# An RWKV layer with a gated FFN on 8 cores: first transfers, prologue order and the first units of token chunk 1

## The chip, the cores and the metric

The kernel runs on one Trainium2 chip, on all 8 NeuronCores, with one program. Core b takes batch element b and shares nothing with the others but the memory that the weights are read from. A core has a matrix engine (PE), a vector engine (DVE), a scalar engine (ACT), a general engine (POOL), a queue engine that only starts transfers (SP), and 16 DMA engines that all queues feed. The metric is the device time in microseconds of the slowest core.

## What is computed

Each core has x of 4096 tokens by 1024 channels.

```python
xn = _layernorm(x, axis=-1)
x = x + attn(xn) + ffn(xn)

# attn: k = xn Wk^T, r = xn Wr^T, v = r, w = -exp(time_decay), u = time_first
y = wkv_scan(w, u, k, v)          # a recurrence over the tokens, by channel
out = sigmoid(r) * y
attn = out @ Wo^T

# ffn, weights of integers times 1/127, hidden size 3072
ffn = (silu(xn @ Wgate^T) * (xn @ Wup^T)) @ Wdown^T
```

## The kernel before

**Chunks and units.** The tokens are cut into 8 chunks of 512 (`TC`), each of 4 tiles of 128 tokens (`NT`). A *unit* of projection work is two accumulation groups of 8 matmuls of 512 columns, into the two banks of one of three PSUM pairs (`pair`). A "gu" unit is 128 hidden channels of gate (line 309) and up (line 313); a "kr" unit is 128 channels of k (line 309) and r (line 313). Its weight tile is 1 MB of int32 or float32 in memory, is cast to a bfloat16 tile of 512 KB by a POOL transfer (line 262), and goes to one of four ring buffers (`R = 4`). Chunks 0 and 1 are worked in pairs, so that each weight tile is read once for both: `GU` and `KR` list the units in order, and `gu 0, 1, 2` are chunk 0 and `gu 3, 4, 5` are the same three weight tiles for chunk 1. SP writes each cast tile back to memory in bfloat16 (line 200) for chunks 2 to 7.

**Layer norm of a tile.** SP loads 128 rows of x (`x_load`, line 170, 512 KB). DVE takes the statistics (`ln_bn`: two `BATCH_NORM_STATS2` and an aggregate), ACT makes the reciprocal deviation (`ln_rstd`: Ln, drain, Exp), DVE the bias (`ln_nb`), ACT the normalised tile (`ln_xt`, line 381, into one of two `xt` buffers). PE transposes it with 8 matmuls of 128 columns (`tr`, line 291), and ACT and DVE copy one bank each into `xn` (`ln_ev`, lines 397 and 503). Chunks 0 and 1 (tiles 0 to 7) are done so in the prologue.

**After a unit.** For a gu unit ACT takes the silu of the gate bank (`gate`, line 420) and DVE multiplies (`ffn_h`, line 549, which raises `v_h` and so frees the PSUM pair). For a kr unit DVE takes the maximum (`att_max`), ACT three exponentials (`att_exp`), DVE the product (line 521, which raises `v_zA` and frees the pair) and two scans (`att_scan`), then `att_den`, ACT the reciprocal (`att_rec`: Ln and Exp), and DVE `att_out`. There is one buffer each of `ek`, `zA` and `den`.

**What sets the order.** Every engine's stream is written out by hand, and waits are on counting semaphores. `SLOTS` lists what takes the PSUM pairs in turn: slot q uses pair q % 3, and `acquire` waits until slot q - 3 has been read. Before the change the transposes have slots too. PE's prologue is `tr(0..3)`, gu 0, `tr(4)`, gu 1, `tr(5)`, gu 2, `tr(6)`, `tr(7)`, kr 0, and from there on three gu units and a kr unit in turn. SP issues x tiles 0 to 7, the two small tables `tdt` and `tft`, and three tiles of x for the residual sum (`res_load`), all without a wait. POOL waits for x tile 3 (`xl3`, line 255) and then issues the first four weight tiles; a later one waits for its ring buffer (`unit_done`) and for the write-back of what was in it (`wb_done`). After the projections of chunks 0 and 1 come, by chunk, the output units (lines 327 and 334) and the projections of the later chunks.

## Time and profile before

| | before |
|---|---|
| time, median of 3 runs | 1359.35 us (1358.83 to 1359.63) |
| the profiled execution's own time | 1359.52 us |
| its span, slowest core (core 3) | 1358.0 us |
| spans of cores 0 to 7 | 1356.6, 1357.7, 1356.3, 1358.0, 1355.6, 1357.1, 1357.8, 1357.7 us |
| PE busy | 1334.7 us (98%) |
| DVE, ACT, POOL busy | 674.6, 396.5, 35.2 us |
| granted TensorE clock, all cores | 1.00 |

The span goes from the first to the last instruction of a core. The time of the execution is 1.5 us longer than the span of its slowest core. A PE that is 98% busy leaves some 23 us in which it is not, and the 40 slices of the page put nearly all of that into the first slice. So the views to read are those of the prologue: the chain of waits, the instructions in order of time, and the transfers.

### The profile page before, as it was taken

To read this page: it belongs to the slowest core of one execution; us is meant where nothing else is said; L and a number is where in the kernel's file an instruction comes from. 1 tells how busy PE (TensorE), PEld (TensorE's weight loads), DVE (VectorE), ACT (ScalarE), POOL (GpSimd) and SP (SyncE) were. 2 spreads that over 40 slices of the span, in tenths; PEclk is the share of its full clock that TensorE was granted. 3 is DMA by queue.
4 is the path that set the end of the run, shared out by engine and by line. 5 is a ranking of instruction groups with operands and counts; after the bars stand their busy time and mean duration, and the time that the engine had idled before them with its cause. 6 is when DMAs were issued, how large, how long until landed. Compare 5 with 4: busy or idle time off the path is not lost.

```text
span 1358.0 us, 17854 instructions; the slowest of 8 cores (1355.6 to 1358.0 us)
## 1 busy us (share of the span) xinstructions
PE 1334.7 (98%) x6208; PEld 606.6 (45%) x6208; DVE 674.6 (50%) x1101; ACT 396.5 (29%) x663; POOL 35.2 (3%) x70
## 2 busy tenths in 40 slices
PE   4999999999999999999999999999999999999999
PEld 2444444444444444444444444444444444444444
DVE  4666666515952288323873238721487215672211
ACT  5554545312331233212332123221233212221100
POOL 0111111000000000000000000000000000000000
PEclk9999999999999999999999999999999999999999
DMA  9699989953554544545545444544455443334411
GB/s 231 144 183 196 209 163 181 204 142 120 167 144 148 168 137 135 147 150 176 125 117 163 155 156 124 143 152 156 150 143 126 155 155 124 94 102 164 153 47 55
DMA packets 90376, 200.41 MB, mean 148 GB/s; under 512 B 32816, under 2 KB 35888, under 8 KB 90160
## 3 DMA queue, kind: packets, MB, share of 16 engines
q1 hardware_dynamic: 55584, 167.81, 39.0%
q0 software_dynamic: 9360, 25.17, 12.5%
q10 hardware_dynamic: 25344, 6.29, 2.5%
q8 instruction: 51, 0.84, 0.2%
q14 instruction: 37, 0.30, 0.1%
HBM read 184.56 MB, written 33.55 MB: 161 GB/s over the span
## 4 chain that ended last, share of the span: by engine, by line
PE 98%; DMA 2%; SPq 0%; issue 0%; DVE 0%; DVEq 0%; POOLq 0%
PE ps L309 33%; PE ps L313 33%; PE ps_o L327 24%; PE ps_o L334 8%; DMA ring<-w_gu 1%; DMA x_buf<-x_tm 1%; PE ps L291 0%; SPq L170 0%; DVE xres L556 0%; DVEq L555 0%; POOLq L255 0%
## 5 line engine op out<-in xcount | busy, mean ns | idle before, releaser
L309 PE MATMUL ps<-xn,ring 128*128 128x512 bf16 x2048 | 485.5, 380 | 4.1 <-DMA ring<-w_gu 3.9
L313 PE MATMUL ps<-xn,ring 128*128 128x512 bf16 x2048 | 484.7, 379 | 0.0
L549 DVE SCALAR_TENSOR_TENSOR h_act<-ps,silu 128x512 bf16<-128x512 f32 x192 | 132.5, 690 | 438.4 <-PE ps L313 427.5
L327 PE MATMUL ps_o<-wd_bf,h_act 128*128 128x512 bf16 x1536 | 342.0, 379 | 0.0
L309 PEld LDWEIGHTS ps<-xn,ring 128*128 128x128 bf16 x2048 | 200.5, 98 | 246.1 <-issue 6.2
L313 PEld LDWEIGHTS ps<-xn,ring 128*128 128x128 bf16 x2048 | 200.7, 98 | 242.6 <-issue 1.7
L420 ACT ACTIVATE silu<-ps 128x512 f32<-128x512 f32 x192 | 114.6, 597 | 452.7 <-PE ps L309 452.4
L327 PEld LDWEIGHTS ps_o<-wd_bf,h_act 128*128 128x128 bf16 x1536 | 150.3, 98 | 181.3
L334 PE MATMUL ps_o<-wo_bf,outp 128*128 128x512 bf16 x512 | 120.9, 379 | 0.0
L402 ACT ACTIVATE den<-den 128x512 f32<-128x512 f32 x64 | 40.3, 630 | 260.1 <-DVE den L537 259.9
L556 DVE TENSOR_TENSOR xres<-xres,ps_o 128x512 f32<-128x512 f32 x64 | 44.0, 688 | 87.0 <-PE ps_o L334 86.4
L523 DVE TENSOR_TENSOR_SCAN SAB<-ewv,SAB,zA 128x512 f32<-128x512 f32 x64 | 82.3, 1285 | 5.9
L525 DVE TENSOR_TENSOR_SCAN SAB<-ewv,SAB,ek 128x512 f32<-128x512 f32 x64 | 80.6, 1260 | 0.0
L509 DVE TENSOR_REDUCE kmax<-ps 128x1 f32<-128x512 f32 x64 | 44.0, 688 | 72.9 <-PE ps L309 72.9
L334 PEld LDWEIGHTS ps_o<-wo_bf,outp 128*128 128x128 bf16 x512 | 50.1, 98 | 60.4
L521 DVE TENSOR_TENSOR zA<-ek,ps 128x512 f32<-128x512 f32 x64 | 43.9, 686 | 15.0 <-ACT enr L413 15.0
L531 DVE SCALAR_TENSOR_TENSOR den<-ek,euv,SAB 128x512 f32<-128x512 f32 x64 | 48.1, 752 | 6.1 <-issue 0.4
L533 DVE SCALAR_TENSOR_TENSOR zA<-zA,euv,SAB 128x512 f32<-128x512 f32 x64 | 47.7, 746 | 0.0
L537 DVE SCALAR_TENSOR_TENSOR den<-enr,den 128x512 f32<-128x512 f32 x64 | 44.3, 692 | 5.2
L543 DVE TENSOR_TENSOR outp<-zA,den 128x512 bf16<-128x512 f32 x64 | 44.0, 688 | 4.9 <-ACT den L404 4.9
L488 DVE BATCH_NORM_STATS2 bnst<-x_buf 128x6 f32<-128x512 f32 x56 | 35.8, 682 | 16.7 <-DMA x_buf<-x_tm 16.7
L411 ACT ACTIVATE ek<-ps,nm 128x512 f32<-128x512 f32 x64 | 42.8, 669 | 0.0
(40 smaller groups left out, 319.1 us busy)
## 6 DMA issues: line engine op xcount, KB each, us to landing
ring<-gu_bfd SPq DMA_DIRECT2D x144, 512.0 KB, 3.3
ring<-kr_bfd SPq DMA_DIRECT2D x48, 512.0 KB, 3.9
xres<-x_tm SPq DMA_DIRECT2D x64, 256.0 KB, 5.5
out_tm<-xres SPq DMA_DIRECT2D x64, 256.0 KB, 4.7
x_buf<-x_tm SPq DMA_DIRECT2D x28, 512.0 KB, 6.4
ring<-w_gu POOLq DMA_DIRECT2D x24, 512.0 KB, 11.3
gu_bfd<-ring SPq DMA_DIRECT2D x24, 512.0 KB, 7.4
ring<-w_kr POOLq DMA_DIRECT2D x8, 512.0 KB, 7.4
```

Of the source, the lines that this page charges most:

```text
L309: ins = te.matmul(bank(kind, idx, 0), w[:, gc * D:(gc + 1) * D], xn[c % 2][:, gc, :], start=(gc == 0), stop=(gc == G - 1))
L313: ins = te.matmul(bank(kind, idx, 1), w[:, C + gc * D:C + (gc + 1) * D], xn[c % 2][:, gc, :], start=(gc == 0), stop=(gc == G - 1))
L327: te.matmul(ps_o[i % 2], h_act[c % 2][:, hg * TC + tt * D:hg * TC + (tt + 1) * D], wd_bf[:, half, hg * 512:(hg + 1) * 512], start=(hg == 0 ...
L334: ins = te.matmul(ps_o[i % 2], outp[c % 2][:, g * TC + tt * D:g * TC + (tt + 1) * D], wo_bf[:, half, g * 512:(g + 1) * 512], start=False, ...
L420: sc.activation(out=silu[i % 3], in_=bank("gu", i, 0), func=Act.Silu, scale=1.0 / 127.0).then_inc(sem["s_sil"], 1)
L509: ve.reduce_max(kmax[:, g:g + 1], bank("kr", a, 0), axis=AX)
L523: ve.tensor_tensor_scan(out=SAB[:, 0, 1:TC + 1], data0=ewv[:, g:g + 1].to_broadcast([D, TC]), data1=zA, initial=SAB[:, 0, 0:1], op0=Alu.mu ...
L525: ve.tensor_tensor_scan(out=SAB[:, 1, 1:TC + 1], data0=ewv[:, g:g + 1].to_broadcast([D, TC]), data1=ek, initial=SAB[:, 1, 0:1], op0=Alu.mu ...
L531: ve.scalar_tensor_tensor(out=den, in0=ek, scalar=euv[:, g:g + 1], in1=SAB[:, 1, 0:TC], op0=Alu.mult, op1=Alu.add)
L533: ve.scalar_tensor_tensor(out=zA, in0=zA, scalar=euv[:, g:g + 1], in1=SAB[:, 0, 0:TC], op0=Alu.mult, op1=Alu.add)
L537: ve.scalar_tensor_tensor(out=den, in0=enr, scalar=1.0, in1=den, op0=Alu.add, op1=Alu.mult).then_inc(sem["v_den"], 1)
L549: ve.scalar_tensor_tensor(out=h_act[c % 2][:, hg * TC:(hg + 1) * TC], in0=bank("gu", i, 1), scalar=1.0 / (127.0 * 127.0), in1=silu[i % 3], ...
```

## The change

Four things change, all but one before the first kr unit.

*Transfers.* SP issues x tiles 0 to 3 at once, tiles 4 and 5 when tile 3 has landed, tiles 6 and 7 when the second weight tile has; the three residual tiles come after the write-back of weight tile 8. `tdt` and `tft` are issued by ACT, as its first instructions. POOL starts the first four weight tiles when x tile 1 has landed instead of x tile 3.

*PSUM.* The transposes leave `SLOTS`. They use the output banks `ps_o` and, for tiles 1 and 3, pair 2; each bank of a transpose is waited for by itself.

*PE.* The first three gu units of chunk 1 are split by tokens, in `gu_part`: tokens 0 to 255 right after gu 2, between the transposes 6 and 7, and tokens 256 to 511 behind that. kr 0 and kr 1 follow, one behind the other. From gu 6 on the order is as before.

*DVE and ACT.* The statistics, bias and normalisation of a tile follow one another by tile, `etd` and `wv` are made at the start, and tiles 6 and 7 come behind the first gates. `att_max(1)` stands behind `att_den(0)`.

```diff
-SLOTS = [("tr", l0) for l0 in range(NT)]
-SLOTS += [("gu", 0), ("tr", 4), ("gu", 1), ("tr", 5), ("gu", 2), ("tr", 6), ("tr", 7), ("kr", 0)]
-for s0 in range(1, 2 * G):
+SLOTS = [("gu", i0) for i0 in range(6)] + [("kr", 0), ("kr", 1)]
+for s0 in range(2, 2 * G):
...
+        def tr_bank(l, k):
+            return pair[2][k] if l in (1, 3) else ps_o[k]
...
-                for l in range(2 * NX):
+                for l in range(NX):
                     x_load(l)
-                sy.dma_start(out=tdt, in_=td_hbm).then_inc(sem["io_td"], 16)
-                sy.dma_start(out=tft, in_=tf_hbm).then_inc(sem["io_tf"], 16)
-                for i in range(3):
-                    res_load(i)
+                sy.wait_ge(*x_landed(3))
+                x_load(NX)
+                x_load(NX + 1)
+                sy.wait_ge(*loaded(1))
+                x_load(NX + 2)
+                x_load(NX + 3)
...
+                            if n == 8:
+                                for i in range(3):
+                                    res_load(i)
...
-                gp.wait_ge(sem["xl3"], 16)
                 for n in range(NS):
+                    if n == 0:
+                        gp.wait_ge(*x_landed(1))
...
+                def evacuated(l, k):
+                    te.wait_ge(sem["v_ev" if k else "s_ev"], l + 1)
...
                 def tr(l):
-                    acquire("tr", l)
                     te.wait_ge(sem["s_xt"], l + 1)
                     for cb in range(G):
+                        if l >= 2 and cb % 4 == 0:
+                            evacuated(l - 2 if l < 5 else l - 1, cb // 4)
...
+                def gu_part(i, t0, t1):
+                    c = GU[i][0]
+                    if t0 == 0:
+                        acquire("gu", i)
+                        te.wait_ge(*loaded(RING_AT[("gu", i)]))
+                    w = ring[RING_AT[("gu", i)] % R]
+                    for m in range(2):
+                        for gc in range(G):
+                            if m == 0 and gc % 4 == 0:
+                                evacuated(NT * c + t1 - 1, gc // 4)
+                            ins = te.matmul(bank("gu", i, m)[:, t0 * D:t1 * D],
+                                            w[:, m * C + gc * D:m * C + (gc + 1) * D],
+                                            xn[c][:, gc, t0 * D:t1 * D],
+                                            start=(gc == 0), stop=(gc == G - 1))
+                        if t1 == NT:
+                            ins.then_inc(sem["t_u" if m else "t_g"], 1)
...
                 proj("gu", 2, 0, "t_g", "t_u")
+                gu_part(3, 0, 2)
                 tr(6)
+                gu_part(4, 0, 2)
                 tr(7)
-                proj("kr", 0, 0, "t_k", "t_r")
-                xn_ready(1)
-                for s in range(1, 2 * G):
+                gu_part(5, 0, 2)
+                for i in range(3, 6):
+                    gu_part(i, 2, NT)
+                for s in range(2):
+                    proj("kr", s, s, "t_k", "t_r")
+                for s in range(2, 2 * G):
```

Three places show how the engines' streams move. In the names, `ps0_0` is the first bank of pair 0, `ps_o0` an output bank, `ring0` a ring buffer; the semaphores `xl3` and `xl1` are the landing of x tiles 3 and 1, `ldc0` that of the first weight tile, and `v_h`, `v_zA` the freed pairs.

PE behind gu 2, before: the two transposes, kr 0, then the first unit of chunk 1.

```order
L291 MATMUL ps0_0<-ident,xt0 128x128 [waits v_h,s_xt]
L291 MATMUL ps0_0<-ident,xt0 128x128 x3
L291 MATMUL ps0_1<-ident,xt0 128x128 x4
L291 MATMUL ps1_0<-ident,xt1 128x128 [waits s_ev,v_ev,s_xt]
L291 MATMUL ps1_0<-ident,xt1 128x128 x3
L291 MATMUL ps1_1<-ident,xt1 128x128 x4
L309 MATMUL ps2_0<-xn0,ring3 128x512 [waits v_h,ldc3]
L309 MATMUL ps2_0<-xn0,ring3 128x512 x7
L313 MATMUL ps2_1<-xn0,ring3 128x512 x8
```

PE behind gu 2, after: half a unit, transpose 6, and the next half.

```order
L331 MATMUL ps0_0<-xn1,ring0 128x256 [waits v_h,ldc0,s_ev]
L331 MATMUL ps0_0<-xn1,ring0 128x256 x3
L331 MATMUL ps0_0<-xn1,ring0 128x256 [waits v_ev]
L331 MATMUL ps0_0<-xn1,ring0 128x256 x3
L331 MATMUL ps0_1<-xn1,ring0 128x256 x8
L295 MATMUL ps_o0<-ident,xt0 128x128 [waits s_xt,s_ev]
L295 MATMUL ps_o0<-ident,xt0 128x128 x3
L295 MATMUL ps_o1<-ident,xt0 128x128 [waits v_ev]
L295 MATMUL ps_o1<-ident,xt0 128x128 x3
L331 MATMUL ps1_0<-xn1,ring1 128x256 [waits v_h,ldc1,s_ev]
```

Transpose 6 now stands behind half a unit, and kr 0 is no longer behind transpose 7.

ACT behind the first transposed tile of chunk 1, before: `xt` of tile 6 (`xt0`) comes after one gate.

```order
L420 ACTIVATE silu0<-ps1_0 128x512 [waits t_g]
L397 CAST xn1<-ps2_0 128x4x128 [waits t_tr]
L381 ACTIVATE xt0<-wd_bf,nbias0,rstd0 128x1024 [waits t_tr,v_nb]
L420 ACTIVATE silu1<-ps0_0 128x512 [waits t_g]
L397 CAST xn1<-ps1_0 128x4x128 [waits t_tr]
L381 ACTIVATE xt1<-wd_bf,nbias1,rstd1 128x1024 [waits t_tr,v_nb]
L420 ACTIVATE silu2<-ps2_0 128x512 [waits t_g]
```

ACT at the same place, after: tile 6 comes behind all three gates, with its reciprocal deviation.

```order
L446 ACTIVATE silu0<-ps0_0 128x512 [waits t_g]
L423 CAST xn1<-ps_o0 128x4x128 [waits t_tr]
L446 ACTIVATE silu1<-ps1_0 128x512 [waits t_g]
L446 ACTIVATE silu2<-ps2_0 128x512 [waits t_g]
L396 ACTIVATE lnv0<-mv0,eps_t 128x1 [waits v_bn]
L398 ACTIVATE rstd0<-lnv0 128x1
L407 ACTIVATE xt0<-wd_bf,nbias0,rstd0 128x1024 [waits t_tr,v_nb]
```

The Ln and Exp of tile 6 moved from ahead of the first gate to behind the third.

PE behind the first three units of chunk 1, after: kr 0 and kr 1, then gu 6 to gu 8. Before, only kr 1 stood here.

```order
L313 MATMUL ps0_0<-xn0,ring3 128x512 [waits v_h,ldc3]
L313 MATMUL ps0_0<-xn0,ring3 128x512 x7
L317 MATMUL ps0_1<-xn0,ring3 128x512 x8
L313 MATMUL ps1_0<-xn1,ring3 128x512 [waits v_h,ldc3]
L313 MATMUL ps1_0<-xn1,ring3 128x512 x7
L317 MATMUL ps1_1<-xn1,ring3 128x512 x8
L313 MATMUL ps2_0<-xn0,ring0 128x512 [waits v_h,ldc0]
L313 MATMUL ps2_0<-xn0,ring0 128x512 x7
L317 MATMUL ps2_1<-xn0,ring0 128x512 x8
L313 MATMUL ps0_0<-xn1,ring0 128x512 [waits v_zA,ldc0]
L313 MATMUL ps0_0<-xn1,ring0 128x512 x7
L317 MATMUL ps0_1<-xn1,ring0 128x512 x8
```

The unit behind these, gu 8, takes the pair of kr 1 and waits for `v_zA` of kr 1; before, two units stood between a kr unit and the one that takes its pair as well, but no other kr unit came right ahead of it.

## Rows read from the trace of the kernel before

**Rows 1.** Waits of PE over the whole span, core 3: total us, times, longest.

```profile
PE ps L291 <- ACT xt L381: 16.0, 4, 11.5
PE ps L309 <- DMA ring<-w_gu: 3.9, 1, 3.9
PE ps L309 <- issue: 0.2, 1, 0.2
```

**Rows 2.** Chain that ended last, core 3, 0 to 42 us: start, us, what.

```profile
2.44 9.43 DMA x_buf<-x_tm
...
12.48 11.33 DMA ring<-w_gu
...
23.94 3.57 PE ps L309 x8
27.51 2.55 PE ps L313 x8
30.06 0.45 PE ps L291 x8
30.51 1.73 PE ps L309 x8
```

**Rows 3.** Instructions in order of time, core 3, layer norm: start, us, engine, line.

```profile
5.83 1.29 DVE L488 BATCH_NORM_STATS2 bnst<-x_buf 128x6 f32<-128x512 f32 x2 [4.46 <-DMA x_buf<-x_tm]
...
7.48 1.28 ACT L370 ACT_TABLE_LOAD   x1 [7.48 <-DVE mv L491]
...
8.78 0.29 ACT L370 ACTIVATE lnv<-mv,eps_t 128x1 f32<-128x1 f32 x1
9.14 0.20 ACT L372 ACTIVATE rstd<-lnv 128x1 f32<-128x1 f32 x1
...
9.47 0.15 DVE L497 SCALAR_TENSOR_TENSOR nbias<-mv,rstd 128x1 f32<-128x1 f32 x1
...
10.12 1.22 ACT L381 ACTIVATE xt<-x_buf,nbias,rstd 128x1024 bf16<-128x1024 f32 x1
...
11.49 1.01 PE L291 MATMUL ps<-ident,xt 128*128 128x128 bf16 x8 [11.49 <-ACT xt L381]
...
12.61 0.69 DVE L503 CAST xn<-ps 128x512 bf16<-128x512 f32 x1 [1.42 <-PE ps L291]
```

**Rows 4.** Chain that ended last, core 0, 18 to 25 us.

```profile
22.10 0.56 issue
```

**Rows 5.** Landing of the x tiles, line 170, core 3, 0 to 70 us.

```profile
DMA to landing us min/median/max: 4.7/10.0/13.0
```

**Rows 6.** Instructions in order of time, core 3: the gate of gu 2.

```profile
36.23 0.60 ACT L420 ACTIVATE silu<-ps 128x512 f32<-128x512 f32 x1
```

**Rows 7.** Instructions in order of time, core 3, 40 to 55 us: work behind kr 0.

```profile
40.91 0.69 DVE L509 TENSOR_REDUCE kmax<-ps 128x1 f32<-128x512 f32 x1 [1.05 <-PE ps L309]
41.67 0.16 DVE L511 SCALAR_TENSOR_TENSOR nm<-kmax,nm 128x1 f32<-128x1 f32 x1
...
43.21 0.29 ACT L409 ACTIVATE esb<-nm 128x1 f32<-128x1 f32 x1
...
44.67 0.69 DVE L521 TENSOR_TENSOR zA<-ek,ps 128x512 f32<-128x512 f32 x1 [0.78 <-ACT enr L413]
...
46.65 1.26 DVE L525 TENSOR_TENSOR_SCAN SAB<-ewv,SAB,ek 128x512 f32<-128x512 f32 x1
...
48.60 0.75 DVE L531 SCALAR_TENSOR_TENSOR den<-ek,euv,SAB 128x512 f32<-128x512 f32 x1
...
50.17 0.69 DVE L537 SCALAR_TENSOR_TENSOR den<-enr,den 128x512 f32<-128x512 f32 x1
...
53.87 0.63 ACT L404 ACTIVATE den<-den 128x512 f32<-128x512 f32 x1
```

**Rows 8.** Chain that ended last, core 1, 0 to 42 us.

```profile
24.84 3.16 PE ps L309 x8
```

**Rows 9.** Instructions in order of time, core 1, POOL.

```profile
13.11 1.76 POOL L262 DMA_DIRECT2D ring<-w_gu  x3 [11.30 <-DMA x_buf<-x_tm]
```

## What the change should do to the time: the prediction

> **What bounds the kernel now.** I read the waits of PE first. Over the whole span PE waits in three places only: 16.0 us for normalised tiles before the first four transposes, 3.9 us for the first weight tile, and 0.2 us of its own issue [rows 1]. All of it lies before 39 us; no weight tile after the first is ever waited for. So an edit can gain only by letting PE begin its first projection earlier, and whatever PE waits anew counts in full. The chain that ended last shows what sets that beginning, 23.94 us: four x tiles land by 11.87, POOL, which waits for the last of them, issues the first weight tile at 12.48, and it lands 11.33 later, at 23.81 [rows 2]. From there PE runs without a gap that matters to the end. Its first unit takes 3.57 + 2.55 us where a later one takes 2 x 1.73: 2.7 us more, since its matmuls start at half the rate [rows 2]. I leave that as it is.
>
> **The earlier weight tile.** POOL now waits for x tile 1. DVE can start on that at about 8 us, so the first weight tile is issued some 4.4 us sooner. With the same 11.33 us to landing it is there at 19.4 or, with x tiles 4 to 7 and the residual tiles no longer ahead of it, sooner. The weight tile stops being the last to come; what comes last instead is the layer norm of tile 3.
>
> **The layer norm of tiles 0 to 3.** DVE now finishes a tile before it starts the next. One tile's round is: statistics, 5.83 to ACT's start at 7.48, 1.65 us; Ln and Exp, 8.78 to 9.34, 0.56; the bias 0.15 and hops of about 0.15 [rows 3]. That is 2.5 us a tile. Making `etd` early moves ACT's table load of 1.28 us [rows 3] beside the first statistics, if `tdt` has landed by about 5.9; I take that as so. Tile 3's statistics then start at 5.83 + 3 x 2.5 + 0.7 (the cast of tile 0 ahead of it) = 14.0, when it has long landed (11.87). Onward: 1.65 + 0.56 + 0.25 to the bias, 16.5; the normalisation 0.1 + 1.22, 17.8; hop and transpose 0.15 + 1.01, 19.0; the cast 0.1 + 0.69, 19.8 [rows 3]. The new code also puts more single waits in PE's stream. On core 0 PE starts 0.56 us after the last cast ended [rows 4], with four waits behind one another there, so 0.14 each; two or three of them give 0.3. First projection at **20.1 us**, against 23.94: 3.8 us gained. The bound on the other side is the weight tile still last at 11.33 + 8.4 = 19.7, which is no later.
>
> **Transposes 6 and 7.** From 20.1, gu 0, tr 4, gu 1, tr 5, gu 2 take 6.12 + 0.45 + 3.45 + 0.45 + 3.45 = 13.9 [rows 2]: gu 2 ends at 34.0. Half a unit later, at 35.75, PE wants transpose 6. But ACT makes tile 6 ready only behind the gate of gu 2. A gate starts 0.1 after the first half of its unit and takes 0.60 [rows 6]: 33.0. Then the table of Ln and Exp must be loaded again, 1.28, the pair 0.56, DVE's bias 0.25, the normalisation 1.32 and the hop 0.15 [rows 3]: 36.55. A new wait of **0.8 us**. Tile 7's statistics follow on DVE at 35.1, and 1.65 + 0.56 + 0.25 + 1.32 + 0.15 later, at 39.0, transpose 7 can start; PE is there at 36.55 + 0.45 + 1.73 = 38.75: **0.3 us**. Behind these wait the half units of gu 4 and 5. Before, both tiles had their statistics and their reciprocal deviation done ahead of the first gate, and PE waited for neither.
>
> **The half units.** 96 matmuls of 256 columns take the place of 48 of 512. Columns are the same; a transpose matmul of 128 columns goes through in 0.45 / 8 = 0.056 us [rows 2] with its own weight load, so a load for 256 columns is hidden. I take 0 for them, and 0.3 us for waits between them, bounded by 0 and by 0.14 for each of the ten or so, 1.4.
>
> **kr 1 right behind kr 0.** gu 8 takes the pair of kr 1 and waits for its product `zA`. In the clock of the trace before, kr 0's first half ends just before 40.91 and kr 0 at 42.5; kr 1, gu 6 and gu 7 end 10.4 later, at 52.9. DVE and ACT have: maximum to 41.83, product of kr 0 to 45.36, scans to 47.91, then the `den` group, 48.60 to 50.86 in the trace, 2.26 long, now at once: 50.2. Only then comes the maximum of kr 1 (0.92): 51.2. ACT first owes the reciprocal of kr 0, two activations of 0.63 from 50.3: 51.65. From the start of the exponentials to the product are 43.21 to 44.67, 1.46, and the product takes 0.69 [rows 7]: 53.8, and PE goes at 53.9. New wait: **1.0 us**. The units behind it find their pairs free by 0.2 us or more, and the lag is gone by kr 3. Before, a kr unit had three gu units between it and the next, and PE did not wait there [rows 1].
>
> **Transfers in the rest.** The residual tiles now load beside later weight tiles. Since none of those was waited for [rows 1], I take 0, from 0 to 1.5 us. The weight tiles for gu 8 and kr 2 have two to three us more than before between issue and use, as kr 1 and the half units stand there.
>
> **The sum**, on core 3: 3.8 gained; 0.8 + 0.3 + 0.3 + 1.0 lost, and the 0.2 of issue gone: net 1.6 us, a span of 1356.4. The metric is the slowest core. Cores that did not wait for a weight tile gain less, as core 0 shows, where the cast was last [rows 4], and the slow start of PE has another length on each: on core 1 its first eight matmuls took 3.16, not 3.57 us [rows 8]. With spans of 1356 to 1357 on most cores, I put the slowest at 1356.9, 1.1 below the 1358.0 before. The profiled execution took 1359.52 for a median of 1359.35, so I carry the difference over: **1358.2 us**. A change of 0.2% is 2.7 us, about what a measurement of this kernel can tell from none; the forecast is within it.
>
> **Rivals.**
> *The new waits do not come* (17%). If tile 6 is ready in time and kr 1's product too, only the gain at the start is left, 3.8 on core 3 and some 3.5 at the slowest: 1355.6. For it: both waits are short, under 1.1 us, beside chains of ten steps. Against it: each chain is a sum of rows, and the table load alone is larger than the wait at transpose 6.
> *The weights slow x tiles 2 and 3* (15%). The weight tiles are now issued at 8 us while x tiles 2 and 3 are still in flight. On core 3 tile 3 has 2 us to spare (11.87 against 14.0). On core 1 it landed at 13.1, as POOL's issue shows [rows 9]; two streams over the same 16 engines from 10 us on would put it at 16.1, and from there 6.1 us go to the first projection: 22.2, where it was 24.84 [rows 8]. Core 1 gains 2.6 and loses 2.4: nothing is left, and by it the time is 1359.3, up to 1361 if the tile is later still.
> The Trainium skill, "DMA: Bandwidth & Descriptors", in its section "Queues, rings and completion order", has each DMA engine go round the queues it has work for, a packet at a time; by that, early weights do take bandwidth from the x tiles, and core 1's case is the rule rather than the exception. No row of before has both in flight in this stretch, so it stays a rival.
> *Tiles 6 and 7 late* (7%, slower). They are issued only when weight tile 1 has landed, by estimate some 3 us behind the first, 22 to 23, and share the engines with weight tiles 2 and 3 and two write-backs. An x tile took 4.7 to 13.0 us to land [rows 5]. At 13.0 tile 6 is there at 35.5, and 1.65 + 0.56 + 0.25 + 1.32 + 0.15 later, at 39.4, its transpose, 2.9 behind the forecast. It decides from a landing at 37.5 on: then transpose 6 is 4.9 late and the time 1363.
> *The first weight tile does not come sooner* (3%): the start stays at 23.9, the new waits stay too: 1361.6.
> *The forecast* has 58%.
>
> **How the numbers follow.** Faster by over 0.2% is below 1356.6: the first rival and a tail of the forecast, 0.20. Slower by over 0.2% is above 1362.1: the third rival, a bit of the fourth, 0.08. Same: 0.72. The range leaves the far ends of the first and the third out: 1355.6 to 1361.2.
>
> **What would show it.** First projection on core 3 near 20 us, released by a cast and not by a weight tile. A wait of PE before transpose 6 released by ACT `xt`, with a table load right ahead on ACT, 0.8 us. A wait of about 1 us on the second gu unit behind gu 6, released by DVE line 554 (`zA`). If PE waits at the half units for DMA, or x tile 3 lands after 14 us, the second or third rival holds. If ACT's first table load still stands behind the first statistics, `tdt` came late and the start is up to 1.3 us later. If the sum of PE's new waits is under 1 us, I was too dear and the change is faster.

## The result, and the profile after

The change makes the kernel slower.

| | before | after |
|---|---|---|
| median | 1359.49 us | 1366.31 us |
| range of the runs | 1358.83 to 1359.96 | 1365.91 to 1366.48 |
| ratio, 95% interval | | 1.005 (1.0033 to 1.0068) |
| span, slowest core | 1358.0 us (core 3) | 1364.7 us (core 5) |
| spans of the eight cores | 1355.6 to 1358.0 | 1362.1 to 1364.7 |

The forecast was 1358.2 us with a range up to 1361.2; the time lies 8.1 us above the one and 5.1 above the other. All medians and ranges, here and below, leave out the executions in which the cores of one die or both ran some per cent slower at a lower granted clock, whatever the kernel.

Waits of PE over the whole span, kernel after, core 5: total us, times, longest. There were six in [rows 1]; here are nine:

```profile
PE ps_o L295 <- ACT xt L407: 15.2, 4, 8.7
PE ps L295 <- ACT xt L407: 5.3, 2, 3.2
PE ps_o L295 <- ACT xn L423: 1.5, 1, 1.5
PE ps L313 <- DVE zA L554: 1.1, 1, 1.1
PE ps L313 <- DVE xn L536: 1.0, 1, 1.0
```

The same core in order of time, the steps that the prediction spoke of:

```profile
9.43 1.76 POOL L268 DMA_DIRECT2D ring<-w_gu  x3 [7.62 <-DMA x_buf<-x_tm]
...
11.62 10.92 SPq L170 DMA_DIRECT2D wd_bf<-x_tm  x4
...
20.70 3.57 PE L313 MATMUL ps<-xn,ring 128*128 128x512 bf16 x8 [1.05 <-DVE xn L536]
...
23.44 1.29 DVE L521 BATCH_NORM_STATS2 bnst<-wd_bf 128x6 f32<-128x512 f32 x2 [3.00 <-DMA wd_bf<-x_tm]
...
27.59 0.61 PE L295 MATMUL ps_o<-ident,xt 128*128 128x128 bf16 x8 [1.51 <-ACT xt L407]
...
28.41 1.29 DVE L521 BATCH_NORM_STATS2 bnst<-wd_bf 128x6 f32<-128x512 f32 x2 [2.41 <-DMA wd_bf<-x_tm]
...
33.12 0.61 PE L295 MATMUL ps_o<-ident,xt 128*128 128x128 bf16 x8 [1.46 <-ACT xn L423]
```

The first projection starts at 20.70, released by a cast and no longer by a weight tile; on the eight cores it is 20.27 to 20.75, where it was 22.30 to 24.84. That part came as forecast. Then DVE waits for x tiles 4 and 5, which [rows 1 to 3] gave no hint of: in the kernel before, the statistics of these two start at 15.44 and 18.48 on core 3 with no wait. Here they start at 23.44 and 28.41, and PE waits 1.51 us before transpose 4 and 1.46 before transpose 5.

The third new wait is the largest. What leads to transpose 6:

```profile
31.07 1.24 ACT L407 ACTIVATE xt<-wd_bf,nbias,rstd 128x1024 bf16<-128x1024 f32 x1 [0.42 <-DVE nbias L530]
...
32.41 0.56 ACT L423 CAST xn<-ps_o 128x512 bf16<-128x512 f32 x1
32.99 1.28 ACT L446 ACT_TABLE_LOAD   x1
...
34.28 0.60 ACT L446 ACTIVATE silu<-ps 128x512 f32<-128x512 f32 x1
...
36.26 0.68 DVE L582 SCALAR_TENSOR_TENSOR h_act<-ps,silu 128x512 bf16<-128x512 f32 x1
36.86 1.28 DVE L521 BATCH_NORM_STATS2 bnst<-wd_bf 128x6 f32<-128x512 f32 x2
...
38.49 1.28 ACT L396 ACT_TABLE_LOAD   x1 [2.14 <-DVE mv L524]
...
40.78 1.24 ACT L407 ACTIVATE xt<-wd_bf,nbias,rstd 128x1024 bf16<-128x1024 f32 x1 [0.43 <-DVE nbias L530]
...
42.28 1.01 PE L295 MATMUL ps_o<-ident,xt 128*128 128x128 bf16 x8 [3.35 <-ACT xt L407]
...
43.08 3.62 PE L331 MATMUL ps<-xn,ring 128*128 128x256 bf16 x16
```

Late tile 5 holds ACT, ACT's cast and table load hold the first gate, the gates hold DVE's `ffn_h`, and DVE takes the statistics of tile 6 only behind two of them. From the statistics of tile 5 to transpose 6 it is 13.86 or 13.87 us on each of the eight cores, though tile 5's statistics start anywhere from 26.99 to 28.94, and PE waits 3.35 us on each. So transpose 6 comes 13.87 us behind the statistics of tile 5, whatever PE did before. The half unit behind it takes 3.62 us; the one ahead of it took 1.91. The granted clock says why (stretch, its length, busy time and instructions by engine, then PEclk, the DMA share and GB/s):

```profile
38.00:42.00 4.00, 0.92 (x9) 0.59 (x6) 2.40 (x7) 3.00 (x4) 0.00 (x0) 0.92 0.00 0
42.00:43.00 1.00, 0.72 (x8) 0.75 (x9) 0.20 (x1) 0.52 (x3) 0.00 (x0) 0.50 0.00 0
43.00:46.50 3.50, 3.50 (x20) 2.44 (x19) 0.85 (x2) 1.71 (x2) 0.00 (x0) 0.50 0.00 0
46.50:50.00 3.50, 3.50 (x30) 3.06 (x29) 0.69 (x1) 0.59 (x1) 0.00 (x0) 0.76 0.00 0
50.00:54.00 4.00, 4.00 (x40) 3.58 (x38) 1.29 (x2) 2.37 (x3) 1.28 (x3) 1.00 0.00 0
```

PE had stood still for 3.35 us before transpose 6, and the granted clock is 0.50 (1.2 GHz) from there to 46.5, and 1.00 (2.4 GHz) again from 50. The page of the profile has the same in its first line: PE is busy 1337.5 us where it was 1334.7, with the same columns.

Last, the unit behind gu 6 and gu 7, as forecast:

```profile
69.83 1.89 PE L313 MATMUL ps<-xn,ring 128*128 128x512 bf16 x8 [1.09 <-DVE zA L554]
```

**Where the time went.** From start to start of PE's groups in the two traces, core 5 after against core 3 before (each the slowest of its kernel):

| stretch of PE | before | after | difference |
|---|---|---|---|
| start of the first projection | 23.94 | 20.70 | -3.24 |
| gu 0, up to transpose 4 | 5.96 | 6.89 | +0.93 |
| transpose 4 to transpose 5 | 3.90 | 5.53 | +1.63 |
| standing still before transpose 6 | 0 | 3.54 | +3.54 |
| transpose 6 to kr 0 | (9.64 at full clock) | 12.48 | +2.84 |
| rest, up to the end of kr 0 and gu 3 to 5 | | | -0.21 |
| wait before gu 8 | 0 | 1.09 | +1.09 |
| sum | | | +6.58 |

The 9.64 are 2 transposes of 0.46, a half unit of 1.74 and 64 matmuls in 6.98 us, as an experiment below shows them at full clock. The spans differ by 6.7. On this pair of cores the start gained 3.2 us, on core 3 alone 3.67 of the 3.8 forecast, and 9.8 us were lost behind it. The ledger says where PE lost time, not which edit made it lose it; for that there are the experiments.

### The profile page after: what moved, and what is told of

It reads as the page before. It is cut to its first block, busy times and chain, and to the rows that moved or that the text cites. A ratio compares the mean times of both kernels' runs of the same rounds, so it can differ in the third digit from the quotient of the medians.

```text
span 1364.7 us, 17958 instructions; the slowest of 8 cores (1362.1 to 1364.7 us)
## 1 busy us (share of the span) xinstructions
PE 1337.5 (98%) x6256; PEld 612.5 (45%) x6256; DVE 674.9 (49%) x1101; ACT 396.4 (29%) x663; POOL 35.1 (3%) x70
## 4 chain that ended last, share of the span: by engine, by line
PE 96%; DMA 2%; ACT 1%; DVE 1%; issue 0%; DVEq 0%; SPq 0%; ACTq 0%
PE ps L313 31%; PE ps L317 31%; PE ps_o L348 24%; PE ps_o L355 8%; DMA wd_bf<-x_tm 1%; PE ps L331 1%; DMA x_buf<-x_tm 1%; DVE bnst L521 0%; PE ps_o L295 0%; SPq L170 0%; DVE zA L554 0%; DVEq L523 0%; ACT xt L407 0%; DVE SAB L556 0%; ACT L396 0%
## 5 line engine op out<-in xcount | busy, mean ns | idle before, releaser
L313 PE MATMUL ps<-xn,ring 128*128 128x512 bf16 x2024 | 479.8, 380 | 2.1 <-DVE zA L554 1.1
L317 PE MATMUL ps<-xn,ring 128*128 128x512 bf16 x2024 | 478.3, 379 | 0.0
L313 PEld LDWEIGHTS ps<-xn,ring 128*128 128x128 bf16 x2024 | 198.0, 98 | 241.5 <-issue 4.5
L317 PEld LDWEIGHTS ps<-xn,ring 128*128 128x128 bf16 x2024 | 198.1, 98 | 239.3 <-issue 0.8
L428 ACT ACTIVATE den<-den 128x512 f32<-128x512 f32 x64 | 40.3, 630 | 266.2 <-DVE den L570 266.0
## 6 DMA issues: line engine op xcount, KB each, us to landing
ring<-w_gu POOLq DMA_DIRECT2D x24, 512.0 KB, 11.1
```

What stands on the lines that cost most here:

```text
L313: ins = te.matmul(bank(kind, idx, 0), w[:, gc * D:(gc + 1) * D], xn[c % 2][:, gc, :], start=(gc == 0), stop=(gc == G - 1))
L317: ins = te.matmul(bank(kind, idx, 1), w[:, C + gc * D:C + (gc + 1) * D], xn[c % 2][:, gc, :], start=(gc == 0), stop=(gc == G - 1))
```

## Experiments: who makes x tiles 4 and 5 late

**All x tiles at once.** The kernel after, but SP issues x tiles 0 to 7 without a wait.

```diff
-                for l in range(NX):
+                for l in range(2 * NX):
                     x_load(l)
-                sy.wait_ge(*x_landed(3))
-                x_load(NX)
-                x_load(NX + 1)
-                sy.wait_ge(*loaded(1))
-                x_load(NX + 2)
-                x_load(NX + 3)
```

> The changed kernel, but SP issues x tiles 0 to 7 at once, without the two waits; all else as changed. Theory A (the four early weight tiles hold back x tiles 4 and 5, which land at 23.4 and 28.4 us on core 5 instead of 14; ACT and DVE wait for them in order, PE waits 1.5, 1.5 and 3.35 us before transposes 4, 5 and 6, and its clock falls to half behind the last): tiles 4 and 5 are there before 20 us, the first two waits go, the third shrinks to 1 us or less, the granted clock stays at 1.00, and the time is 1358 to 1359.5 us. Rival B (the new order itself makes tile 6 late: its statistics and table load stand behind the gates): the wait of 3.35 us and the fall of the clock stay, only the first two waits go, about 1363 us.

Measured: 1362.8 us (9 runs, 1361.98 to 1363.80), ratio 1.0026 (1.0016 to 1.0036), the time of rival B. 3.5 us come back, and no core waits at transposes 4 and 5. DVE on core 0, in order of time (no transfer ends a wait any more), then ACT and PE:

```profile
20.52 1.28 DVE L515 BATCH_NORM_STATS2 bnst<-wd_bf 128x6 f32<-128x512 f32 x2
23.41 1.29 DVE L515 BATCH_NORM_STATS2 bnst<-wd_bf 128x6 f32<-128x512 f32 x2 [0.35 <-issue]
...
33.07 0.69 DVE L576 SCALAR_TENSOR_TENSOR h_act<-ps,silu 128x512 bf16<-128x512 f32 x1 [0.55 <-ACT silu L440]
...
35.32 1.28 ACT L390 ACT_TABLE_LOAD   x1 [1.17 <-DVE mv L518]
...
39.10 0.61 PE L289 MATMUL ps_o<-ident,xt 128*128 128x128 bf16 x8 [2.17 <-ACT xt L401]
...
39.65 2.86 PE L325 MATMUL ps<-xn,ring 128*128 128x256 bf16 x16
```

Transpose 6 still waits, 2.17 us on every core, with all tiles there: that is order alone. The chain now begins at transpose 5: transpose 6 follows it by 7.98 or 7.99 us on all eight cores, and PE has 5.8 us of work in between. Behind this wait too the clock fell (the half unit takes 2.86 us here, and from transpose 6 to kr 0 it is 11.3 to 11.6 us on the eight cores). Half of the loss is held tiles, half is not.

**The other end: old order, new transfers.** The kernel before with the diff's transfers alone: tiles held, POOL at x tile 1, `tdt` and `tft` by ACT, residual tiles at n = 8.

```diff
-                gp.wait_ge(sem["xl3"], 16)
                 for n in range(NS):
+                    if n == 0:
+                        gp.wait_ge(*x_landed(1))
```

> The kernel before, with only the new transfers: POOL starts the weights at x tile 1, SP holds back x tiles 4 to 7, the small tables go out from ACT, the residual tiles behind weight tile 8. Theory A: in the old order DVE takes the statistics of tiles 4 and 5 ahead of the last casts of chunk 0, so the first projection has to wait for x tile 5, 28 us, and comes at about 30 us, 6 us later than before: 1365 us or more. Rival B (the transfers are harmless, the order costs): the first projection no later than before, 1358 to 1360 us.

Measured: 1369.2 us (4 runs), ratio 1.0071 (1.0056 to 1.0086). Core 1:

```profile
23.86 1.29 DVE L496 BATCH_NORM_STATS2 bnst<-wd_bf 128x6 f32<-128x512 f32 x2 [6.07 <-DMA wd_bf<-x_tm]
29.36 1.29 DVE L496 BATCH_NORM_STATS2 bnst<-wd_bf 128x6 f32<-128x512 f32 x2 [3.18 <-DMA wd_bf<-x_tm]
```

That is theory A. The old order has the statistics of tiles 4 and 5 ahead of the casts of tile 3, so the first projection itself waits, to 33.83 (29.41 to 33.85 by core). The tiles are late at much the same times as in the kernel after, with another order: the transfers make them late. The whole is 9.7 us slower than before; in the new order the late tiles cost 3.5, so it hides the larger part.

**Weights 1 to 3 stepped back.** The kernel after, but POOL issues only the first weight tile at x tile 1, and the next three when x tile 5 has landed.

```diff
                     if n == 0:
                         gp.wait_ge(*x_landed(1))
+                    if n == 1:
+                        gp.wait_ge(*x_landed(5))
```

> The changed kernel with one wait more: POOL issues only the first weight tile at x tile 1, and the other three when x tile 5 has landed. Everything else, the held x tiles too, as changed. Theory A (the weight tiles that are not needed yet take the engines from x tiles 4 and 5): x tiles 4 and 5 land by 19 to 20 us instead of 22 to 24 and 27 to 29, PE's waits before transposes 4 and 5 go, the one before transpose 6 falls from 3.35 to the 2.2 us of e1, and the time is 1362 to 1363.5 us, if the weight tiles behind come in time. Rival (holding the x tiles back is what makes them late, whatever the weights do): tiles 4 and 5 still land after 23 us and the time stays at 1366.

Measured: 1365.5 us (4 runs, 1365.03 to 1365.57), ratio 1.0046 (1.0031 to 1.0061): a miss by 2. Core 4:

```profile
11.21 16.09 SPq L170 DMA_DIRECT2D wd_bf<-x_tm  x4
...
19.95 1.06 POOL L270 DMA_DIRECT2D ring<-w_gu  x2 [10.21 <-DMA wd_bf<-x_tm]
...
23.34 1.29 DVE L523 BATCH_NORM_STATS2 bnst<-wd_bf 128x6 f32<-128x512 f32 x2 [0.36 <-issue]
35.75 1.29 DVE L523 BATCH_NORM_STATS2 bnst<-wd_bf 128x6 f32<-128x512 f32 x2 [2.23 <-DMA wd_bf<-x_tm]
```

Tile 5 has landed by 19.95, and no statistics of tiles 4 and 5 wait for a transfer (they start at 20.43 and 23.34). In the kernel after, those of tile 5 start at 26.99 on this core, behind a wait of 2.28 us for it. So a tile issued at 11 us is late only with several weight tiles in front of it, and with early weights a tile is late only if it is issued behind them: either edit alone brings tiles 4 and 5 in time. But SP holds x tiles 6 and 7 for the landing of weight tile 1, which now comes later: SP's group of four ends at 27.3, and tile 6's statistics start at 35.75, waiting for the transfer, where it was 35.44 on this core in the kernel after. Transpose 6 waits 4.5 to 5.3 us on four cores, 3.8 on one and 2.2 to 3.3 on the other three; on the two of these where DVE did not wait for tile 6 it is 2.2, as with all tiles at once. My expectation had moved one wait and not looked at what hangs on it.

**Early normalisation, tiles still held.** The kernel after with DVE's and ACT's work on tiles 6 and 7 moved ahead of the first gates (the edit stands in the next section).

> The changed kernel with its own transfers and the order of e6 for tiles 6 and 7. Theory: with tiles 6 and 7 landing at 30 to 34 us this order is worse, since the casts of tile 4 and the gates stand behind them: PE waits some 6 us before transpose 5, and the time is 1368 us or more. Rival (the order alone was the cost, the transfers were not): 1363 us or less.

Measured: 1366.9 us, in one run (spans 1361.4 to 1365.3), too few to compare. In its trace the wait before transpose 4 is 3.2 to 5.3 us, where I had expected 6 before transpose 5: DVE takes the statistics in turn, ahead of work that could go. There is no sign that this order is better while tiles are held.

## Experiments: what the order costs

**The clock.** The kernel after with 14 matmuls of 512 columns ahead of transpose 6, that no one reads.

```diff
                 gu_part(3, 0, 2)
+                evacuated(5, 0)
+                for k in range(14):
+                    te.matmul(ps_o[0], ident, xn[0][:, 0, :], start=True, stop=True)
                 tr(6)
```

> The changed kernel with 14 matmuls of 512 columns put in front of transpose 6, whose result the transpose overwrites: they fill 3.0 us of the 3.35 us wait, so the wait is nearly gone in name but nothing behind it comes sooner. Theory A: the clock does not fall, transpose 6 and the half unit behind it run at 0.45 and 1.73 us instead of 1.01 and 3.4, transpose 7 too: 2.2 us less than the changed kernel, 1364.1 us. Rival (the fall of the clock costs nothing on the path, since ACT and DVE set the pace of transpose 7 as well): 1366.3 us, no change.

Measured: 1365.0 us (4 runs, 1364.80 to 1365.12), ratio 1.004 (1.0025 to 1.0055): 1.3 us back where 2.2 were expected. Core 1:

```profile
39.74 3.19 PE L371 MATMUL ps_o<-xn,ident 128*128 128x512 bf16 x14
43.25 0.61 PE L295 MATMUL ps_o<-ident,xt 128*128 128x128 bf16 x8 [0.33 <-ACT xt L410]
43.71 1.91 PE L331 MATMUL ps<-xn,ring 128*128 128x256 bf16 x16
46.12 0.61 PE L295 MATMUL ps_o<-ident,xt 128*128 128x128 bf16 x8 [0.49 <-ACT xn L426]
46.58 7.15 PE L331 MATMUL ps<-xn,ring 128*128 128x256 bf16 x64
```

The granted clock stays at 1.00 on all cores. From transpose 6 to kr 0 it is 10.3 us on six cores and 10.5 on two, where the kernel after has 10.9 to 12.7. Two things can have taken the difference; the traces show both, but no run parts them. PE at full speed now waits 0.5 us for a cast of tile 6. And the cores do not all lose the same: in the kernel after, the cores with the latest transpose 6 (core 7 at 42.81, core 1 at 42.41) take 11.1 and 11.3 us, and cores 0, 5 and 6, with an earlier one, 12.5 to 12.7. Without the fall the first kind is the slowest, as core 1 is here. The metric takes the maximum, and to it the clock is worth 1.3 us and not 2.2.

**Transpose 4 to pair 2.** In the kernel after, transposes 4 and 5 take the same banks, so transpose 5 waits for a cast of tile 4 and not for its own `xt`.

```diff
-            return pair[2][k] if l in (1, 3) else ps_o[k]
+            return pair[2][k] if l in (1, 3, 4) else ps_o[k]
```

(with the waits for the casts moved accordingly, and one ahead of gu 2.)

> The kernel after, but transpose 4 goes to PSUM pair 2 instead of the output banks that transpose 5 takes too, and gu 2 waits for its casts. It asks whether the waits of PE before the transposes 5 and 6 add up. In the kernel after, transpose 5 waits 1.46 us for ACT's cast of tile 4 (on core 5 to 33.12), while its own xt is ready at 32.31. Theory (the waits are stations of one chain through ACT and DVE that ends at xt of tile 6): transpose 5 goes up to 0.8 us earlier, the wait before transpose 6 grows by the same amount, 3.35 to some 4, and the time stays at 1366.3, within 0.3. Rival (each wait has a price of its own): the wait before transpose 6 stays at 3.35 and the time falls by 0.7 to 1365.6.

Measured: 1366.7 us (5 runs, 1365.95 to 1367.12), ratio 1.0049 (1.0036 to 1.0062): nothing gained, as the theory said. Core 1:

```profile
32.80 0.61 PE L295 MATMUL ps_o<-ident,xt 128*128 128x128 bf16 x8 [0.97 <-ACT xt L409]
...
42.51 1.01 PE L295 MATMUL ps_o<-ident,xt 128*128 128x128 bf16 x8 [3.59 <-ACT xt L409]
```

The wait before transpose 6 is 3.56 to 3.72 us on the eight cores, not 3.35, and from tile 5's statistics to transpose 6 it is 13.87 us as before (13.87 to 13.89 on six cores, 14.04 on two). The statistics of tile 5 start at 25.1 to 29.95 here, so this run has later tiles on its slow cores than the kernel after had, and the medians alone would not settle it; the constant 13.87 does. What PE wins before transpose 5, some 0.55 us (4.16 us behind tile 5's statistics instead of 4.71), it gives back: 0.3 ahead of gu 2, which now waits for the casts of tile 4, and 0.2 before transpose 6. Up to transpose 6 the waits in the ledger are stations of one chain through ACT and DVE, and no price list.

**Tiles 6 and 7 ahead of the gates.** All x tiles at once, and the layer norm of tiles 6 and 7 where the kernel before had it. ACT:

```diff
                 ln_rstd(4)
-                ln_xt(4)
                 ln_rstd(5)
+                ln_xt(4)
+                ln_rstd(6)
                 ln_xt(5)
+                ln_rstd(7)
...
-                ln_ev(4)
                 gate(0)
-                ln_ev(5)
+                ln_ev(4)
+                ln_xt(6)
                 gate(1)
+                ln_ev(5)
+                ln_xt(7)
                 gate(2)
-                ln_rstd(6)
-                ln_xt(6)
-                ln_rstd(7)
-                ln_xt(7)
```

and DVE's `ln_bn` and `ln_nb` of 6 and 7 likewise ahead of `ffn_h(0)`. This kernel ran in two series, with an expectation for each.

> As e1 (all x tiles at once), and DVE takes the statistics of tiles 6 and 7, ACT their Ln and Exp, ahead of the first gate, in the pipelined order of the kernel before. Theory: what is left of e1's loss is the wait of 2.17 us before transpose 6, which comes from tile 6 standing behind ffn_h(1) on DVE and behind the gates and a table load on ACT, and the fall of PE's clock behind it, 1 us; both go: about 1359.5 us against 1362.8. Rival (the half units or DVE's load are the cost): 1362 us or more.

> All x tiles issued at once and the layer norm of tiles 6 and 7 ahead of the first gates, the units of the kernel after (half units, kr 1 right behind kr 0): the same kernel as an earlier one whose timed runs were too few. It splits the way from 1362.8 (x tiles at once alone) to 1359.6 (old order of units as well) into tile order and unit order. If the wait before transpose 6 and the clock's fall hold most of it, the median is 1360.3 to 1360.8, and the unit order is worth the 1.09 us of the wait for kr 1's product. If the unit order holds more than that wait, it is 1361.5 or above.

Measured: 1361.1 us in the second series (9 runs, but from 1359.91 to 1364.11), ratio 1.0015 (1.0004 to 1.0026); 1360.49 and 1363.82 in the first, which had two runs. That lies between the two outcomes put down for the second series. The waits before transposes 6 and 7 are gone on all cores. In their place PE waits at transpose 5, before its first half up to 2.4 us for ACT's cast of tile 4 and before its second 0.6 for DVE's, since both stand behind the work on tile 7, and tile 7 comes late when weights and tiles share the engines. On seven cores the clock stays at 1.00. On core 3, which has the longest of these waits and the longest span, it falls (the same columns as in the table of stretches):

```profile
31.88 0.38 PE L289 MATMUL ps_o<-ident,xt 128*128 128x128 bf16 x4 [2.41 <-ACT xn L417]
```

```profile
34.00:36.00 2.00, 2.00 (x6) 0.67 (x5) 0.82 (x2) 1.14 (x2) 0.00 (x0) 0.50 0.54 213
```

From transpose 5's second half to transpose 6 it is 7.1 us there, where PE has 5.4 us of work at full clock. In the first series core 6 had the same fall.

**And the old order of units.** The same, with PE's units as in the kernel before: no half units, kr 0 behind transpose 7, three gu units between it and kr 1.

```diff
                 proj("gu", 2, 0, "t_g", "t_u")
-                gu_part(3, 0, 2)
...
+                tr(6)
+                tr(7)
+                proj("kr", 0, 0, "t_k", "t_r")
+                xn_ready(1)
-                for s in range(2, 2 * G):
+                for s in range(1, 2 * G):
```

(and no call of `gu_part`; transpose 7 goes to pair 1, and `SLOTS` and the streams of ACT and DVE match.)

> As e6, and PE's units in the old order: no halves, kr 0 behind transpose 7, kr 1 behind gu 5. Theory: the wait of 1.1 us on the product of kr 1 goes too, nothing comes in its place, and only the earlier start (20.7 us against 22.3 to 24.8) is left: 1357 to 1358 us, faster than the kernel before by 2. Rival (the first weight tile for kr 0 or tiles 6 and 7 now come last): PE waits before kr 0, no gain over before.

Measured: 1359.6 us (10 runs, 1358.91 to 1362.70), ratio 1.0004 (0.9994 to 1.0013): as the kernel before, and a miss by 2 us for the theory. It is 1.5 us under the version with the new units. The wait for kr 1's product, 1.09 us on every core, is gone with it and can make most of that; the rest is within the spread of 4 us of the other version. What this kernel has of the change is the early first projection (20.0 to 22.75), and it gains nothing by it. Core 6, the slowest:

```profile
19.99 3.23 PE L309 MATMUL ps<-xn,ring 128*128 128x512 bf16 x8 [1.13 <-DMA ring<-w_gu]
...
31.39 0.38 PE L291 MATMUL ps_o<-ident,xt 128*128 128x128 bf16 x4 [2.54 <-ACT xn L414]
32.38 0.38 PE L291 MATMUL ps_o<-ident,xt 128*128 128x128 bf16 x4 [0.60 <-DVE xn L522]
```

Two things hold the gain back. PE waits at transpose 5 on seven of the eight cores, and DVE on all but one for tile 7. And on core 6 alone the clock falls to 0.50 behind these waits (34 to 36 us): gu 2 takes 5.1 us instead of 3.5. In eight of the ten runs the slowest core is one whose mean granted clock is under 1.00.

## Experiments: what the early weights are worth

**POOL back at x tile 3**, once on top of the kernel with all x tiles at once, once on top of the last one.

```diff
+                gp.wait_ge(sem["xl3"], 16)
                 for n in range(NS):
-                    if n == 0:
-                        gp.wait_ge(*x_landed(1))
```

> As e1, and POOL waits for x tile 3 again before the first weight tile: all transfers of the prologue as before the change, but for the small tables and the residual tiles, under the new order. Theory A: the first projection is again released by the weight tile, at 22 to 24 us instead of 20.7; the later waits are those of e1; so 2 to 3 us over e1, about 1361 us. Rival B: the same 2 to 3 us over e1, but from its 1363, about 1366. If the early weight tiles also harm e1, e2 is not slower than e1.

> As e7, and POOL starts the weights at x tile 3 again. It measures what the earlier weight tile is worth by itself where nothing else waits: between e1 and e2 that was 0.9 us. Expected 1 to 2 us over e7, about 1358.5 to 1359 us; if it is 3 us, the prediction's price for the earlier weight was right.

Measured: with the new order 1363.2 us (5 runs, 1362.74 to 1363.85), ratio 1.003 (1.0017 to 1.0043), against 1362.8 with early weights: no difference that counts, where 2 to 3 us had been expected of a later start. With the old order of units 1358.2 us (9 runs, 1357.50 to 1358.86), ratio 0.9991 (0.9981 to 1.0001), against 1359.6: the early weights cost 1.4 us, where I had expected them to bring 1 to 2. Core 3 of the second:

```profile
22.20 3.23 PE L308 MATMUL ps<-xn,ring 128*128 128x512 bf16 x8 [3.08 <-DMA ring<-w_gu]
```

It starts its first projection at 20.7 to 22.8, on core 3 1.4 us later than the kernel with early weights, waits there for the weight, and behind that for 0.3 us at most: tiles 5 to 7 are on time. The clock stays up in all its runs but for one core in one. The early start was bought with late tiles, and more than all of it went back.

**The small tables.** `tdt` and `tft` are 4 KB each. The kernel before, with ACT issuing them first, as the change has it, and nothing else:

```diff
-                sy.dma_start(out=tdt, in_=td_hbm).then_inc(sem["io_td"], 16)
-                sy.dma_start(out=tft, in_=tf_hbm).then_inc(sem["io_tf"], 16)
...
+                sc.dma_start(out=tdt, in_=td_hbm).then_inc(sem["io_td"], 16)
+                sc.dma_start(out=tft, in_=tf_hbm).then_inc(sem["io_tf"], 16)
                 sc.wait_ge(sem["v_c"], 1)
                 ln_rstd(0)
```

> The kernel before, with only the two small tables (2 x 4 KB) issued by ACT as its first instructions instead of by SP behind the x tiles. Theory: in the kernels with this edit the first x tile lands at 4.7 to 8.8 us, in the kernel before at 4.4 to 6.3; the small transfers go between those of x tile 0, and x tile 0 comes up to 2.5 us late on a core. Then the first statistics start at over 6.5 us on some cores here too, and the time is 0 to 1 us over the kernel before, as the first weight tile waits for x tile 3 and not for tile 0. Rival (it is chance between cores and runs): 4.4 to 6.3 as before and no change, 1359.5 us.

Measured: 1361.1 us (9 runs, 1359.70 to 1361.51) against 1359.1 of before on that chip, ratio 1.0012 (1.0002 to 1.0022). Cores 0 and 3:

```profile
6.75 1.29 DVE L488 BATCH_NORM_STATS2 bnst<-x_buf 128x6 f32<-128x512 f32 x2 [5.38 <-DMA x_buf<-x_tm]
```

```profile
4.80 1.29 DVE L488 BATCH_NORM_STATS2 bnst<-x_buf 128x6 f32<-128x512 f32 x2 [3.43 <-DMA x_buf<-x_tm]
```

The statistics of x tile 0 start at 4.76 to 6.75 us by core here, where before it was 4.44 to 6.29. In every other trace with the tables on ACT some core has it at 6.5 to 8.8; in the four with them on SP (before, and the three kernels below) none is later than 6.4. It is a small cost: the interval nearly touches 1, and the first of the two kernels below, which takes this edit back, is as far under the kernel before as the one without (1.1 us). Nor does this trace show where 2 us would go: its own time is 1359.9 us, and its first projections start at 22.97 to 24.45, none later than before (24.84). In the kernel after it cost nothing at the start: tile 0 is at 4.73 on core 5 and at 6.40 on core 0, tile 1 at 8.92 and 8.84, and the first projection at 20.70 and 20.63.

**Tables back on SP**, behind the x tiles, on the best kernel so far; ACT loads its table by an exponential of a constant instead. Once with POOL at x tile 3, once with the first weight tile at x tile 1 and three more at x tile 5.

```diff
-                sc.dma_start(out=tdt, in_=td_hbm).then_inc(sem["io_td"], 16)
-                sc.dma_start(out=tft, in_=tf_hbm).then_inc(sem["io_tf"], 16)
                 sc.wait_ge(sem["v_c"], 1)
-                sc.wait_ge(sem["io_td"], 16)
-                sc.activation(out=etd, in_=tdt, func=Act.Exp).then_inc(sem["s_etd"], 1)
+                sc.activation(out=warm, in_=eps_t, func=Act.Exp)
```

(`etd` and `wv` are made behind the work on tile 7 instead.)

> As e9 (new layer norm order, old order of units, all x tiles at once, weights at x tile 3), with the two small tables issued by SP behind the x tiles, their two small operations back behind tile 7, and the load of the Ln and Exp table started early by an operation on a constant. Theory: x tile 0 lands by 6.3 us on all cores, but the first weight tile still sets the start, so at most 0.5 us under e9: 1357.8 to 1358.3 us.

> As e10, and the weights staggered: the first at x tile 1, the other three when x tile 5 has landed. It is meant to keep both gains, the early weight tile and the undisturbed x tiles: first projection at 20 to 20.5 us, released by the layer norm and not by a weight tile, no wait before transposes 4 to 7. 1356 to 1357 us, faster than the kernel before by 0.2%. If the weight tiles of gu 1 or gu 2 then come last, PE waits for DMA behind gu 0 or gu 1, and the time is that of e10 or above.

Measured: 1358.05 us (8 runs), ratio 0.999 (0.998 to 1.000), as expected, and 1357.8 us (7 runs), ratio 0.9993 (0.9982 to 1.0004), where 1356 to 1357 had been expected. The second starts its first projection at 19.3 to 20.5, the first at 20.7 to 22.5, and they end alike: transpose 7 starts at 35.0 to 36.1 in the second and at 35.1 to 36.5 in the first. In the second PE waits again at transpose 5, up to 1.6 us before its first half and 0.6 before its second. So I took that wait away:

**Transpose 4 to pair 2, on this kernel**, by the edit shown above.

> The kernel with the tables back on SP, the first weight tile at x tile 1, the other three at x tile 5 and the old order of units (1358.2), with transpose 4 moved to PSUM pair 2. There the wait before transpose 6 is zero, so transpose 5's waits of 0.6 to 1.4 and 0.6 us on the output bank are on the path. Theory: both vanish, part comes back before transposes 6 and 7 because ACT's order of gates and casts is unchanged; 1357.0 to 1357.6. Rival (ACT's chain sets the end of the prologue whatever the bank): all comes back before transposes 6 and 7, and the time stays at 1358.2.

Measured: 1358.9 us (11 runs, 1357.32 to 1361.66), ratio 0.9996 (0.9986 to 1.0006). Worse by a us, if anything. Core 1, the slowest, and its granted clock right behind (as in the table of stretches above):

```profile
33.17 2.94 PE L314 MATMUL ps<-xn,ring 128*128 128x512 bf16 x8 [3.14 <-DVE xn L528]
```

```profile
34.00:36.00 2.00, 2.00 (x6) 0.71 (x5) 1.02 (x2) 1.17 (x2) 0.00 (x0) 0.50 0.76 293
```

Two short waits before and within transpose 5 became one of 1.5 to 3.1 us ahead of gu 2, for the same cast of tile 4. The chain is ACT's: table load, gate 0, cast. On core 1 ACT also waited 0.64 us for `tft` ahead of the table load; no other core has such a wait on its list. Moving a bank does not shorten the chain, and on two cores the clock falls behind the one wait: on core 1, where it is longest, and on core 3 behind 2.20 us. This too fits one chain, and it is a miss for the theory I had put down, which had the gain at 0.6 to 1.2 us.

None of these versions beats the kernel before by more than its interval; the upper ends of the four fastest are 1.0000 to 1.0006. The best three medians are 1.1 to 1.3 us, 0.1%, below it.

| kernel | us | difference to before, both on one chip |
|---|---|---|
| after | 1366.3 | +6.8 |
| all x tiles at once | 1362.8 | +3.3 |
| and tiles 6, 7 ahead of the gates | 1361.1 | +1.7 |
| and the old order of units | 1359.6 | +0.3 |
| and POOL at x tile 3 | 1358.2 | -1.1 |
| and the tables on SP | 1358.05 | -1.1 |

Each row keeps the edits of the rows above it.

## Why the prediction was wrong

**The start** was right. Forecast 20.1 on core 3, released by a cast; it is 20.27 there and at most 20.75. The price of 2.5 us for a tile's round held (2.44). So did the bound by the weight tile, though its terms were off: the first weight tile is issued at 9.0 on core 3, a microsecond later than I had, and the quickest of the early weight tiles lands in 5.8 us there, not 11.33.

**The step that failed first** is "the weights slow x tiles", which I had as a rival at 15% and for tiles 2 and 3 alone. I took tiles 4 and 5 as on time without pricing them; the text has no term for them. The 13.9 us for gu 0, tr 4, gu 1, tr 5 and gu 2 held no wait at either transpose; on core 5 the stretch took 16.3 (20.70 to 37.01). The tiles are issued at 11.62 and 12.0, when the four weight tiles have just been (POOL, from 9.43 on), and the transfers of that core between 12 and 16 us, and between 16 and 30, are (queue, packets, MB, share of the 16 engines; q0 carries the weights, q1 what SP issues):

```profile
q0 software_dynamic: 147, 0.55, 103.1%
```

```profile
q0 software_dynamic: 394, 1.45, 67.1%
q1 hardware_dynamic: 367, 1.37, 35.0%
```

For four us nothing of the x tiles moves, and after that they have a third (35.9% from 16 to 22 us; behind that q1 also carries write-backs). Tile 5 lands 16.3 us after its issue. Before, the slowest x tile of this core took 14.5 us, but tile 5 was issued at 3.9. So its statistics, 18.52 before, start at 28.41. Not all of that counts. Transpose 6 follows them by 13.87 us, and with all x tiles at once it is at 39.10 on the slowest core; by that, an estimate, tile 5 could have come at 25.2 for nothing, and the 3.2 us beyond are the 3.2 by which transpose 6 is later here (42.28). The Trainium skill ("DMA: Bandwidth & Descriptors", section "Queues, rings and completion order") has the engines go round their queues by packets. I had quoted it, and had looked only at the tiles in flight at that moment, not at those that the change issues behind the weights. From 16 us on the trace agrees with it; the four us before are worse for the x tiles than it says.

**Transpose 6** was right in kind, released by `xt` with a table load ahead of it, and wrong in size: 0.8 forecast, 3.35 measured, 2.17 with all tiles there. I let ACT start Ln of tile 6 as soon as gate 2 was done. But its statistics are on DVE behind `ffn_h(1)`, which waits for gate 1, and gate 1 stands on ACT behind the cast of tile 5. In the trace with all tiles there (core 0) that is 33.07 for `ffn_h(1)`, 33.68 for the statistics and 35.03 for the aggregate; the table load follows at 35.32, and ACT had been idle for 1.17 us. I had followed ACT's stream and not DVE's. From the table load to the transpose it is 3.78 us, where I had 3.56: that part was well priced. The statistics were not in the sum at all.

**Transpose 7**, forecast 0.3: it waits for nothing behind PE's slow stretch; at full clock, in the run with the added matmuls, it waits 0.5, for a cast of tile 6 and not for its own `xt`. **The clock** had no term at all. I had made new waits and priced them at their length. Behind the wait before transpose 6, PE took 10.9 to 12.7 us by core for what it does in 10.3 at full clock, waits included.

**The half units** were right: 64 matmuls of 256 columns take 6.98 us from start to start, 0.109 each, where 0.108 is half of what one of 512 takes. The 0.3 for waits between them did not show. **Transfers in the rest**, taken as 0: seven cores wait for no weight tile behind the start, core 0 for 0.6 us in all.

**gu 8** was right: 1.0 forecast, 1.09 measured, on every core.

**The rivals.** "Tiles 6 and 7 late" had the right side and was the wrong mechanism: the tiles had landed, since DVE takes tile 6's statistics at 36.86 without waiting for a transfer. Its price of 1363 was the nearest of all. No rival had several of these at once, and they were not independent: early weights delay the tiles, late tiles delay the order that was already tight, and behind the wait that comes of it the clock was down. I gave slower 8%, as if each mishap needed a cause of its own.

**Still open.** What held tiles cost with weights at x tile 3, in the new order: that kernel was not run. Why with all tiles at once the early weights cost nothing in one order and 1.4 us in the other. What decides whether the clock falls behind a wait of 2.2 to 2.5 us. And whether the tables on ACT act through their many small packets or through the order of issue was not tried.

## What to carry to other kernels

When transfers are moved ahead of others, price the ones that now stand behind them, one by one, and not only those in flight; and when an engine's work is moved behind another's, follow both streams of the pair, since the later of the two decides. New waits of the matrix engine do not add up: those on one chain swallow each other (the bank moved gained nothing, twice), while a long one can cost more than itself: behind waits of 2.17 to 3.35 us PE lost another 0.6 to 2.4 us in the clock on the cores where it fell. An interval that is the same on all cores, as the 13.87 us from tile 5 to transpose 6, was here the mark of the chain that decides.

## What the runs showed of the hardware

**Who is first holds the DMA engines.** On all eight cores of the kernel after, the weights' queue has 98.5 to 104.3% of the engines' time between 12 and 16 us and the x tiles' queue at most 5.6%, though two tiles had been issued. In the kernel with all x tiles at once it is the other way about: between 10 and 14 us the x tiles have 87% on core 0 and the weights, issued at 8.84, 4%. From there on both share: 62.4 to 40.3% there (14 to 24 us), 67.1 to 35.0% on core 5 of the kernel after (16 to 30 us), more for the casting queue.

**The clock fell behind rather short waits, and not by their length alone.** It was at 0.50 after waits of 3.35 us (kernel after), 3.14 (transpose 4 moved, core 1) and 2.17 us (x tiles at once, core 0: 2.86 us for a half unit). Of two cores of the kernel with transpose 4 moved that both wait 2.20 us before gu 2, core 3 falls to 0.50 (gu 2 takes 5.1 us) and core 4 stays at 1.00 (1.89 us for 8 matmuls). In the first series of the kernel with tiles 6 and 7 ahead of the gates, core 2 waits 2.54 us at transpose 5 and stays at 1.00, and core 6 waits 2.40 and falls. The Trainium skill ("TensorE: Matmul & The Clock Gate", section "What's actually happening") has the half rate as the state of an idle engine; the traces agree in so far as every fall stands behind a wait, though not every wait of this length is followed by one. On the eight cores of the kernel after, the same wait of 3.35 us was followed by a loss of 0.6 to 2.4 us.

**Two transfers of 4 KB, issued first on another queue,** go with an x tile 0 that comes up to 2.5 us later on some cores (8.8 against 6.3 at the latest), and, in the kernel before, with 2.0 us of the whole by the medians (0.3 to 3.0 by the ratio's interval). How the one would lead to the other no trace shows.
